# Dense node products in groups of four tiles, and carried edge sums that enter the node stage by a one-hot product

## What is computed

```
h = x @ W_enc + b_enc                      # L2, also x @ W in L0, L1, L3
ea = edge_attr @ W_ee + b_ee
for i in range(3):
    m = relu(h[src] + ea) * edge_atten
    aggr = segment_sum(m, dst, num_segments=n)
    z = (1.0 + eps[i]) * h + aggr
    z = z @ W1[i] + b1[i]
    z = (z - bn_mean[i]) * rsqrt(bn_var[i] + BN_EPS) * bn_gamma[i] + bn_beta[i]
    z = relu(z) @ W2[i] + b2[i]
    h = relu(z)
```

## Time and profile before

| | us |
|---|---|
| median of 3 runs | 6584.64 |
| lowest and highest | 6583.74, 6596.83 |
| the profiled execution, own time | 6589.41 |
| its span in the trace | 6587.7 |

### The profile page before, as it was taken

How to read it: one execution, slowest core, us unless ns; L and a number is a source line. 1 busy time by engine, 2 the same in 40 slices (tenths; PEclk the granted TensorE clock), 3 DMA queues, 4 the chain that set the end, 5 groups by cost and what they waited for, 6 DMA issues and landing times. The chain is left out here.

```text
span 6587.7 us, 52760 instructions
## 1 busy us (share of the span) xinstructions
PE 3332.1 (51%) x13794; PEld 2046.6 (31%) x13796; DVE 4171.2 (63%) x5389; ACT 1504.4 (23%) x3071; POOL 4147.1 (63%) x4239
## 2 busy tenths in 40 slices
PE   3477777746777776553333333333333333333263
PEld 2355655534555555231111111111112111111231
DVE  5577777766777777554555554555554555555597
ACT  0122222201222221002323232232322232322121
POOL 0477777727777775116777775777775777776220
PEclk7677777776777777775565656656665566665686
DMA  0476666627666664543333332333332333333241
GB/s 21 140 206 194 198 195 195 188 75 205 199 197 197 194 195 121 211 131 100 107 104 104 106 104 82 104 106 104 103 107 82 100 107 103 107 103 102 112 159 60
DMA packets 539815, 878.22 MB, mean 133 GB/s; under 512 B 85125, under 2 KB 382577, under 8 KB 531358
## 3 DMA queue, kind: packets, MB, share of 16 engines
q0 software_dynamic: 167968, 479.61, 25.3%
q1 hardware_dynamic: 371576, 395.35, 18.6%
HBM read 553.95 MB, written 320.67 MB: 133 GB/s over the span
## 5 line engine op out<-in xcount | busy, mean ns | idle before, releaser
L1241 POOL DMA_INDIRECT big<-h_tab,big x2352 | 2224.6, 946 | 815.1 <-issue 815.1
L1281 PE MATMUL psum<-big 128*128 128x512 f32 x1176 | 1085.6, 1078 | 1786.3 <-ACT big L1264 1785.9
L635 POOL DMA_INDIRECT big<-kv_tab,big x1664 | 1648.5, 991 | 533.5 <-issue 497.7
L1307 DVE TENSOR_TENSOR psum<-psum,big 128x1024 f32<-128x1024 f32 x294 | 555.5, 1890 | 1366.2 <-DMA big<-h_tab,big 1366.2
L1281 PEld LDWEIGHTS psum<-big 128*128 128x128 f32 x1176 | 343.1, 322 | 2364.1 <-ACT big L1264 2059.8
L1258 ACT COPY big<-big 128x1024 f32<-128x1024 f32 x294 | 563.4, 1916 | 2102.6 <-DVE big L1301 2102.6
L764 PE MATMUL psum<-big 128*128 128x136 f32 x3328 | 706.6, 364 | 502.3 <-DVE big L822 316.9
L764 PEld LDWEIGHTS psum<-big 128*128 128x128 f32 x3328 | 606.7, 256 | 599.1 <-issue 570.6
L674 ACT COPY big<-psum 125x128 f32<-125x128 f32 x1408 | 376.5, 267 | 1485.8 <-PE psum L720 1415.4
L1301 DVE TENSOR_TENSOR_SCAN big<-big,psum 128x1024 f32<-128x1024 bf16 x294 | 669.0, 2276 | 0.1
L712 PE MATMUL psum<-big 128*128 x4992 | 580.7, 264 | 105.8 <-DVE big L793 105.7
(11 more groups left out here) (389 smaller groups left out, 3295.7 us busy)
## 6 DMA issues: line engine op xcount, KB each, us to landing
run_tab<-big SPq DMA_DIRECT2D x294, 512.0 KB, 2.8
snap_tab<-big SPq DMA_DIRECT2D x176, 448.0 KB
item_tab<-big SPq DMA_DIRECT2D x208, 272.0 KB, 3.9
big<-loc_tab SPq DMA_DIRECT2D x104, 512.0 KB, 4.6
big<-h_tab,big POOLq DMA_INDIRECT x2352, 2.5
big<-kv_tab,big POOLq DMA_INDIRECT x1664, 3.4
snap_tab<-big SPq DMA_DIRECT2D x176, 52.0 KB
kv_tab<-big SPq DMA_DIRECT2D x10, 640.0 KB, 2.9
```

What stands on the lines that cost most here:

```text
L635: nc.gpsimd.indirect_dma_start(out=kv[:, b % SLOTS, k, :], out_offset=None, in_=kv_tab, in_offset=bass.IndirectOffsetOnAxis(ap=src_item[:, ...
L1241: nc.gpsimd.indirect_dma_start(out=got[j % RING][:, k * D:(k + 1) * D], out_offset=None, in_=h_tab, in_offset=bass.IndirectOffsetOnAxis(ap ...
L1281: ins_ = nc.tensor.matmul(bank[2 * (j % DEEP) + k][:, :], ea_T[j % DEEP], w_blocks[:, k * 512:(k + 1) * 512], start=True, stop=True)
L1307: nc.vector.tensor_tensor(by_feature(msg[j % DEEP]), by_feature(msg[j % DEEP]), got[j % RING].rearrange("p (t f) -> p f t", f=D), ALU.add) ...
```

## The change

`node_linear` works in groups of four tiles (`QUADS`: six of four, one of a single tile), all written out with no loop. The transposes read the source directly, ACT's staging copy is gone. Group 0 is transposed before the wait for the weights, and each further group is transposed before the products of the group ahead of it, into two banks in turn; the products have six banks. With 128 columns the four products of a group share a bank and DVE evicts them in one instruction of 512 columns; with 512 columns there are still three evictions for each tile. The writes to `kv_tab` go by groups.

`gine_prep` makes a one-hot matrix `takes` (128 partitions x 3200 columns: which node column the first run of a partition ends in) in place of `first_end`: an IOTA of 3200 columns on POOL instead of one of 1 column, a copy of one column and a compare of 3200 columns on DVE.

`gine_nodes` drops the gather of the first rows, the write back and the wait for it, and POOL starts with the 25 gathers. The carried sums are multiplied with W1 (`carry_w`), and for each group a product of `carry_w` with the 512 columns of `takes` opens the PSUM sum that the product with W1 closes. The groups have four tiles, the staging copy is gone, DVE evicts a group in one instruction and makes `h_plus` from it with the ReLU in the same instruction; the ReLU on `skip` itself is applied by ACT, for all groups behind its other work. The writes to `h_tab` go by groups.

The core of the diff (the removed functions stand above):

```diff
-        def node_linear(sources, loads, cols, parts, tabs):
+        QUADS = [(t, min(t + 4, NT)) for t in range(0, NT, 4)]
+        def node_linear(source, loads, cols, parts, tabs):
...
+                        for lo, hi in QUADS if tabs else ():
+                            sp.wait_ge(evac, evacs_of(hi))
                             for dst, src in tabs:
+                                sp.dma_start(dst[:, lo:hi, :], src[:, lo:hi, :]).then_inc(tab_out, 16)
...
+                        for g, (lo, hi) in enumerate(QUADS):   # ACT
+                            act.wait_ge(tr_done, g + 1)
+                            later(act, mm_done, 4 * (g - 1))
+                            nc.scalar.copy(turned[g % 2][:, 0:(hi - lo) * D], bank[g % 2][:, 0:(hi - lo) * D]).then_inc(copied, 1)
...
+                        def turn(g):                            # PE
+                            lo, hi = QUADS[g]
+                            later(pe, copied, g - 1)
+                            for t in range(lo, hi):
+                                ins_ = nc.tensor.transpose(bank[g % 2][:, (t - lo) * P:(t - lo + 1) * P], source[:, t * D:(t + 1) * D], ident[:, :])
+                            ins_.then_inc(tr_done, 1)
+                        turn(0)
                         pe.wait_ge(w_in, 16 * len(loads))
+                        for g, (lo, hi) in enumerate(QUADS):
+                            if g + 1 < len(QUADS):
+                                turn(g + 1)
+                            pe.wait_ge(copied, g + 1)
...
+                                nc.tensor.matmul(to, turned[g % 2][:, (t - lo) * P:(t - lo + 1) * P], wgt[:, 0:cols], start=True, stop=True).then_inc(mm_done, 1)
...
         def gine_prep():
-                        nc.gpsimd.iota(row0, pattern=[[0, 1]], base=0, channel_multiplier=J, allow_small_or_imprecise_dtypes=True).then_inc(cleared, 1)
+                        nc.gpsimd.iota(takes, pattern=[[1, NT], [NT, P]], base=1, channel_multiplier=0, allow_small_or_imprecise_dtypes=True).then_inc(node_ids, 1)
...
+                        link(nc.vector.tensor_copy(colB[:, 3:4], vn1_nat[:, 0:1]))
...
+                        dve.wait_ge(node_ids, 1)
+                        link(nc.vector.tensor_scalar(takes, takes, colB[:, 3:4], None, ALU.is_equal))
...
         def gine_nodes(layer):
...
+                        for t in range(NT):                     # POOL, its first instruction now
                             nc.gpsimd.indirect_dma_start(out=agg_d[:, t, :], ...
...
+                        def own(g):                             # DVE
+                            dve.wait_ge(g_in[g], 16 * (hi - lo))
+                            nc.vector.scalar_tensor_tensor(z_work3[:, lo:hi, :], skip3[:, lo:hi, :], epsb[:, 3:4], agg_d[:, lo:hi, :], ALU.mult, ALU.add).then_inc(z_ready, 1)
+                        own(0)
+                        for g, (lo, hi) in enumerate(QUADS):
+                            if g + 1 < len(QUADS):
+                                own(g + 1)
+                            dve.wait_ge(m2_done, g + 1)
...
+                        for g, (lo, hi) in enumerate(QUADS):   # ACT, behind its copies and activations
+                            act.wait_ge(h_ready if layer < 2 else biased, g + 1)
+                            nc.scalar.activation(skip[:, lo * D:hi * D], skip[:, lo * D:hi * D], ACT.Relu)
...
+                        pe.wait_ge(w_in, 48)                    # PE
+                        pe.wait_ge(summed, 1)
+                        nc.tensor.matmul(bank[7][:, 0:D], c_t, w1, start=True, stop=True).then_inc(carry_mm, 1)
+                        pe.wait_ge(carry_ready, 1)
...
+                            nc.tensor.matmul(bank[2 + g % 2][:, 0:n], carry_w, takes[:, lo * P:hi * P], start=True, stop=False)
+                            turn(g)
+                            pe.wait_ge(copied, g + 1)
+                            nc.tensor.matmul(bank[2 + g % 2][:, 0:n], w1, z_T[g % 2][:, 0:n], start=False, stop=True).then_inc(m1_done, 1)
+                            pe.wait_ge(y_done, g + 1)
```

More of the change, by code:

```diff
@@ L179, in build @@
         stages = area(o, 4 * U * D)
-        stage_in, stage_in2, stage_T, stage_T2 = (stages[:, k * U * D:(k + 1) * U * D] for k in range(4))
         assert o + 4 * U * D <= BIGW
@@ L1113, in build @@
         b_edge = bias[:, 3 * D:4 * D]
+        takes = area(29512, NT * P)
         ROWS_NAT = P * J
@@ L1457, in build @@
                 loads.append((bias[:, k * D:(k + 1) * D], a[f"L0_{n}_b{c}"].to_broadcast([P, D])))
[L1458 removed]
+            node_linear(src if c == 0 else work, loads, 4 * D,
                         [(q_n, D, 0, D), (kv_n, 2 * D, D, 3 * D), (skip[:, :], D, 3 * D, 4 * D)], [(table(kv_tab), kv_n3)])
```

230 lines of the change are left out of this document (82 added, 148 removed).

## The result

The changed kernel took 6518.65 us (median of four runs, 6518.07 to 6520.61) against 6589.62 for the kernel before beside it (four runs, 6583.74 to 6596.83): ratio 0.9891, 95% interval 0.9879 to 0.9902. Between the two profiled executions, with spans of 6587.7 and 6518.6 us, it is 69.1 us. 41 us were forecast, so the direction and the blocks were right and the size was not.

What follows compares the result with a forecast made beforehand. Blocks run one after another: TensorE paces the wide products, ACT waits weigh on the narrow ones, a TensorE-ACT chain bounds node stages. Gains 12.0 + 17.9 + 11.3 = 41.2 us off 6584.6 give 6543.4 us; range 6528 to 6568.

Steps and rivals of the forecast that it cites:

- the high ends of all of them: Upper gains forecast for the wide calls, narrow calls and node stages: 16, 17.9 and 17 us.
- Wide calls: Two 512-column dense products: ACT waits and staging copy go, final write lands sooner; gain 12.0 us, range 10.6 to 16.
- the reason given for the high end: Wide calls: clock rises one to two us earlier because TensorE no longer stops behind its first transposes; gain 16 us.
- Narrow calls: Three 128-column dense products: waits for ACT go, clock up after 5.4 us; gain 17.9 us, low case 12.7.
- Preparation: Building the one-hot matrix: added POOL and DVE work hidden under 20 us of cover; cost 0.
- Node stages: Three GINE stages: TensorE starts at 8.5 instead of 16.7 us, 4.1 us gained each; 11.3 us in all after ends.
- The reason given for the clock: Node stages: W2, one-hot product and transposes follow without a wait, added matmuls are long; one to two slow groups.
- Rival (a): Node stages: clock mix stays, the added product eats the earlier start, stages -4.6 us; total 6559.3 us, chance 0.22.
- (b): Dense calls gain only half, a new wait replacing the removed one; 15 us less, 6558 us, chance 0.08.
- (c): Node stages: TensorE stays at 1.2 GHz throughout, kernel slower than before; 6588 to 6595 us, chance 0.04.
- (d): Node stages: carry late, weights not there before 8.5 us; 6546 to 6552 us, no separate chance given.
- The rule on the shared port: Node stages: skill warns DVE operations lock GpSimd out, making gathers beside DVE's carry work late; forecast held nothing for it.

Runs made afterwards that it cites:

- h1: Changed kernel with VectorE waiting for all 25 gathers of a node stage before its first group: 6596.22 us, beside 6568.48 for the kernel before.
- h2: As h1, with the seven one-hot products of each node stage left out: 6594.39 us, beside 6568.48 for the kernel before.
- e4: Changed kernel without the one-hot products of the node stages, carried sums missing from the result: ratio 0.9944 to the kernel before.
- i2: The edit of e4 run on another chip, changed kernel without the one-hot products: ratio 0.9925 to the kernel before.
- h3: As h1, with the next group's one-hot product ahead of this group's W2 products: 6576.35 us, beside 6568.48 for the kernel before.
- e6: Changed kernel with the next group's one-hot product issued between this group's W1 and W2 products: 7567.29 us, ratio 0.9915 to the kernel before.
- e7: Changed kernel with the edits of e5 and e6, and ACT's ReLUs inside its loop: ratio 0.9907 to the kernel before.
- e5: Changed kernel with useless added TensorE products during waits at the start of dense calls and node stages: 7572.39 us, ratio 0.9926 to the kernel before.
- a0: The changed kernel itself, run again on a slower chip: 7585.81 us, ratio 0.9937 to the kernel before.

## Why the prediction was wrong, point by point

The forecast missed by 28 us of 69: 3.2 in the wide calls, 7.7 in the narrow ones and 16.9 in the node stages. The mechanisms were right; the terms that failed are the times of short rows of TensorE, in the narrow calls and in the node stage's chain. The result lies below the range of 6528 to 6568 us, whose lower end no term reached either: the high ends of all of them, 16, 17.9 and 17 us, give 6533.7.

**Wide calls.** Right in kind. The pitch of a group was put at 4.08 us (0.88 and 0.14 a tile) and is 3.87; the clock rose 5.9 us into the first call where I had 7.5. TensorE needed 26.9 us in it, not 28.6. Gain 15.2 instead of 12.0 us. It is inside the 10.6 to 16 given, but the reason given for the high end, a clock up one to two us sooner in two calls, is worth 2 us at most and reaches 14.

**Narrow calls.** The term that was mis-sized first: 12.9 us a call forecast, 9.5, 10.5 and 10.7 measured. By starts, four tiles take 0.89 us for the products and 0.44 for the transposes, so 25 tiles with 21 transposed are 7.9 us; I had 10.2, from 0.29 and 0.14 a tile. Those came from dividing the lengths of rows such as the 1.46 us for ten matmuls in the earlier trace rows. Such a row holds two things that a dense series doesn't pay: the ten matmuls that close the changed call, right behind transposes, take 1.28 us (2667.42) where those behind a wait take 1.46, and the last 0.17 us of a row is overlapped by the next (1.06 long, 0.89 from start to start). In short rows the two are much of the row. The clock rose 2.9 us after 2659.23 in the first call where I had 5.4; in the others 5.1 and 5.4. Gain 25.6 instead of 17.9 us, above both ends given, 12.7 and 17.9.

One more thing went with the loop, and the sum did not hold it. In the narrow calls before, the transposes behind a pass start after the end of the products' row (2680.95 + 1.46) and not in its tail:

```profile
2682.48 0.76 PE L1075 MATMUL psum<-ident,big 128*128 128x128 f32 x5
```

That is some 0.2 us a pass at 2.4 GHz. The prediction saw no gap there, in the wide calls, whose matmuls are four times as long. No run tells whether it is the loop's branch.

**Preparation.** Right: 55.1 us after and 55.8 before, from VectorE's first operation to the next block.

**Node stages.** The start was right to 0.1 us (8.5), the step that failed is TensorE's part behind it: 39.1 us forecast with one group at 1.2 GHz, 40.6 by the middle that I took, 35.5, 35.7 and 35.7 measured. Two errors lie in it. The group at 2.4 GHz: forecast 5.56 us with W2 at 1.17 and 0.4 of handoffs; the rows give 1.00 for W2 (3965.94 to 3966.94), 0.86 one-hot, 0.64 transposes, 0.63 copy, 1.17 W1, 0.83 activation, 5.13 in all. So the handoffs come to 0.14 us and not 0.4, and W2, again a short row's length, was 0.17 us too long. With the shorter first and last groups that is 3.6 us a stage. And the clock: I took the middle between one and two slow groups (1.5 us a stage); all three had one. Together 5.1, 4.9 and 4.9 us. The next block begins 3.0, 3.0 and 3.1 us behind TensorE's end where I had 3.7, 3.7 and 3.6, 1.9 us in all. With 0.2 us at the start that is 17 us, the 16.9 by which the term was missed. The high end given, +17, left out the 1.0 us lost at the ends: 15.8.

**The reason given for the clock** was right as far as it names the added work: h1 against h2 show it, and e4 and i2 agree. That the three series follow on one another isn't needed: in h3 the product stands apart from them, in the wait ahead of W2, and the clock rose after one group all the same. It was also the weakest number: without the added product two stages of three stayed low. Rival (a), the clock mix as before, had 0.22; it was more than 40 us away from what came, on the wrong side.

**The rivals.** (b) fell, no wait took the place of the one removed. (c) fell, and h2 shows how far it was: 1.2 GHz throughout is 42.3 us for TensorE's part without the product. (d) fell, the product that waits for the weights starts 3.8 to 4.3 us after the block's start.

**The rule on the shared port.** I held nothing for POOL's gathers being held up by VectorE. In the first two stages after, the 25 gathers took 30.7 us from the first to the last, in the third 30.0. In the first, two of them took 1.36 and 1.25 us instead of 0.95, beside VectorE's fused operation behind the eviction and SP's first write; the third stage has neither. By the Trainium skill, "SBUF — State Buffer", section "SBUF: two separate sides", a VectorE operation with two SBUF inputs and a GpSimd operation that reads SBUF lock each other out of a shared port, which would make such delays. But in e6 and e7 both stand beside the gathers too, and no gather there takes over 1.1 us, so these traces don't bear the rule out. It is 0.7 us and off the path, and no run tells VectorE from SP here.

## What to carry to other kernels

Build a chain from the starts of rows, from one start to the next, and add neither a handoff nor a drain to it: groups summed with the lengths of rows came out 5% (wide), 8% (node stage) and 29% (narrow) too long here, and every error had the same sign. Work added to TensorE in a wait for another engine cost nothing here (groups of 4.26 us in h3 as in h2), and may pay by the clock; work added outside such a wait costs its pitch (5.13 us in h1), and can still pay. A measurement of one change on another chip can have a stall that hides it, so take each block's length from the trace beside the total, and look for the stall in it.

## What was not expected of the hardware

- TensorE's part of a node stage, with equal instructions, took 30.6 us in one stage and 42.3 in the next two of one run (h2), with a granted clock of 0.87 against 0.50.
- A clock raised by useless work fell again within one group, at waits of 2.11, 0.73 and 0.87 us (e5), and was kept where the last of these was filled (e7).
- On three of four chips the same kernel needs 16 to 17% more time. In each node stage there compute engines stand, with the added product until the gathers are through, at 35 us after the first, although what they wait for is done: the transposes of a0's third group were over 10.8 us before ACT began. The profile calls the releaser remote. The cause stays open.
